# Inverse denominators on two sets of partitions, returned by two DMA queues, spread through two row halves of TensorE

## The reference

```python
score = exp(clip((K[src] * Q[dst] / sqrt(dh) * Eh).sum(-1), -5, 5))    # layer 0, 8 heads of 16
wV = segment_sum(V[src] * score, dst)
Z  = segment_sum(score, dst)
h  = x + (wV / (Z + 1e-6)).reshape(N, D)
x1 = layernorm(x + batchnorm(h))
e  = leaky_relu(a_src[src] + a_dst[dst]) ...                           # layer 1: attention, two linears
out = layernorm(x1 + layer1(x1))
```

## Time and profile before

| | before |
|---|---|
| median of three runs | 4573.03 us |
| the profiled execution | 4564.05 us, of which the span from first to last instruction is 4562.0 us |
| mean granted TensorE clock | 0.699 of full speed |
| busy share of the span: PE, DVE, ACT, POOL | 77%, 71%, 26%, 72% |

### The profile page before, as it was taken

The page is one execution under the profiler, slowest core; times in us unless marked ns, Lnnn a source line. Parts: engine busy times, 40 slices in busy tenths (PEclk is TensorE's granted clock), DMA queues, the critical chain, the costliest instruction groups (busy, mean ns, idle before and its releaser), DMA issues. The chain is left out here.

```text
span 4562.0 us, 84765 instructions
## 1 busy us (share of the span) xinstructions
PE 3498.3 (77%) x20796; PEld 2714.5 (60%) x20797; DVE 3235.4 (71%) x9533; ACT 1204.7 (26%) x4817; POOL 3274.2 (72%) x3437
## 2 busy tenths in 40 slices
PE   6787777778778777777889777777777777777778
PEld 5565555556556555565568655655555655556555
DVE  5877878887887878777548666666666666666657
ACT  3111111111111111111234333333333333333325
POOL 4777777777777777776567777777777777777752
PEclk9988988887898888988685555555555555555559
DMA  8666666666666666665343222222222222222224
GB/s 280 195 191 188 194 189 186 191 194 188 191 191 188 187 194 192 190 188 160 101 123 63 61 61 60 59 61 61 61 61 61 59 60 61 61 61 59 61 70 146
DMA packets 432619, 586.92 MB, mean 129 GB/s; under 512 B 210833, under 2 KB 290935, under 8 KB 431079
## 3 DMA queue, kind: packets, MB, share of 16 engines
q0 software_dynamic: 132880, 330.18, 27.5%
q1 hardware_dynamic: 297848, 248.72, 18.5%
q10 hardware_dynamic: 1840, 7.43, 0.4%
HBM read 551.16 MB, written 33.98 MB: 128 GB/s over the span
## 5 line engine op out<-in xcount | busy, mean ns | idle before, releaser
L1099 POOL DMA_INDIRECT xg<-xl_table,idx x1661 | 1590.3, 957 | 518.3 <-issue 498.3
L399 POOL DMA_INDIRECT kv_g<-kv_table,idx x1661 | 1575.4, 948 | 525.3 <-issue 504.5
L1164 PEld LDWEIGHTS ps_sum<-pw,xg 128*128 128x128 f32 x3328 | 741.0, 328 | 164.9 <-DVE pws L1305 164.9
L1164 PE MATMUL ps_sum<-pw,xg 128*128 128x64 f32 x3328 | 819.3, 428 | 3.8 <-DVE pws L1305 2.2
L1151 PE MATMUL ps_tops<-ident,top 128*64 128x128 f32 x832 | 286.1, 447 | 525.5 <-DVE top L1277 525.2
L467 PE MATMUL ps_sum<-kv_g,hot 128*64 128x136 f32 x3328 | 333.0, 328 | 455.8 <-issue 222.0
L449 PE MATMUL ps_pair<-w,eat 128*128 128x128 f32 x3328 | 599.9, 335 | 2.7 <-DMA eat<-in_edges 2.7
L1263 DVE SCALAR_TENSOR_TENSOR ps_lg<-raw 128x256 f32<-128x256 f32 x416 | 185.3, 445 | 573.4 <-ACT raw L1212 566.8
L1212 ACT ACTIVATE raw<-adw,xg 128x64 f32<-128x64 f32 x1664 | 440.8, 336 | 538.0 <-DMA xg<-xl_table,idx 537.8
L449 PEld LDWEIGHTS ps_pair<-w,eat 128*128 128x128 f32 x3328 | 506.5, 233 | 98.3 <-issue 98.3
L467 PEld LDWEIGHTS ps_sum<-kv_g,hot 128*64 128x64 f32 x3328 | 209.7, 154 | 560.8 <-issue 325.5
(11 more groups left out here) (164 smaller groups left out, 4982.5 us busy)
## 6 DMA issues: line engine op xcount, KB each, us to landing
eat<-in_edges SPq DMA_DIRECT2D x416, 256.0 KB
local<-local_table SPq DMA_DIRECT2D x832, 64.0 KB
kv_g<-kv_table,idx POOLq DMA_INDIRECT x1661
xg<-xl_table,idx POOLq DMA_INDIRECT x1661, 2.5
xw<-in_xt SPq DMA_DIRECT2D x416, 32.0 KB
adw<-ad_row SPq DMA_DIRECT2D x416, 32.0 KB, 4.4
kv_table<-kv_out SPq DMA_DIRECT2D x25, 512.0 KB, 5.0
xl_table<-xl SPq DMA_DIRECT2D x25, 264.0 KB, 2.7
```

Of the source, the lines that this page charges most:

```text
L399: nc.gpsimd.indirect_dma_start(out=kv[:, u, k, 0:2 * D], out_offset=None, in_=m["kv_table"], in_offset=bass.IndirectOffsetOnAxis(ap=idx[:, ...
L1099: nc.gpsimd.indirect_dma_start(out=xg[:, u, k], out_offset=None, in_=m["xl_table"], in_offset=bass.IndirectOffsetOnAxis(ap=idx[:, u // B, ...
L1164: nc.tensor.matmul(ps_sum[:, b, 0:W], xg[:, u, k, 0:D], pw[:, b, k], start=(k == 0), stop=(k == K - 1))
```

## The change

A second copy of the inverses stands on partitions 64 to 71 of `acc[:, 1]` (W = 64, H = 8), and `heads` exists on those partitions too. ScalarE returns each piece to partitions 0 to 7 as before, and SyncE returns the same piece to partitions 64 to 71 by a DMA of its own; `inv_back` of a piece counts to 32. Even groups are spread from partitions 0 to 7 and odd ones from 64 to 71. Their PSUM results rotate over the four buffers of `ps_rows`, and a call waits for `divide(g - 4)`. In SyncE's program `return_twin(0)` to `return_twin(2)` stand behind the four L826 DMAs, and `return_twin(3)`, with its wait for the fourth reciprocal, between the first and the second load of `third`.

```diff
-        heads = sb("heads", [H, D])
+        heads = sb("heads", [W + H, D])
+        twin_part = [acc[W:W + H, 1, first * G:end * G].rearrange("h (a n) -> h a n", a=DH) for first, end in DEN_PIECES]
             for piece in range(len(DEN_PIECES)):
                 sp.dma_start(inv_part[piece], den_part[piece]).then_inc(den_out[piece], 16)
+            def return_twin(piece):
+                sp.wait_ge(inverted, piece + 1)
+                sp.dma_start(twin_part[piece], inv_part[piece]).then_inc(inv_back[piece], 16)
+
+            for piece in range(3):
+                return_twin(piece)
             for piece, (first, end) in enumerate(PIECES):
-                sp.wait_ge(inv_back[piece], 16)
+                if piece == 1:
+                    return_twin(3)
+                sp.wait_ge(inv_back[piece], 32)
                 sp.dma_start(third[:, first * G:end * G], xt[:, first * G:end * G]).then_inc(xt_in[piece], 16)
...
             def spread_inv(g):
-                if g >= 2:
-                    pe.wait_ge(divided, g - 1)
-                nc.tensor.matmul(ps_wide[:, g % 2], heads[:], acc[0:H, 1, at(g, G)], start=True, stop=True).then_inc(inv_spread, 1)
+                side = slice(g % 2 * W, g % 2 * W + H)
+                if g >= 4:
+                    pe.wait_ge(divided, g - 3)
+                nc.tensor.matmul(ps_rows[:, g % 4], heads[side], acc[side, 1, at(g, G)], start=True, stop=True).then_inc(inv_spread, 1)
...
-            pe.wait_ge(heads_made, 1)
+            pe.wait_ge(heads_made, 2)
             for piece, (first, end) in enumerate(DEN_PIECES):
-                pe.wait_ge(inv_back[piece], 16)
+                pe.wait_ge(inv_back[piece], 32)
...
-            nc.vector.tensor_copy(heads[:].rearrange("p (b d) -> p b d", d=DH),
-                                  m["ident"][0:H, 0:H].unsqueeze(2).to_broadcast([H, H, DH])).then_inc(heads_made, 1)
+            for side in (0, W):
+                nc.vector.tensor_copy(heads[side:side + H].rearrange("p (b d) -> p b d", d=DH),
+                                      m["ident"][side:side + H, side:side + H].unsqueeze(2)
+                                      .to_broadcast([H, H, DH])).then_inc(heads_made, 1)
...
-                nc.vector.tensor_tensor(part, part, ps_wide[:, g % 2], ALU.mult).then_inc(divided, 1)
+                nc.vector.tensor_tensor(part, part, ps_rows[:, g % 4], ALU.mult).then_inc(divided, 1)
```

## The result

The change made the kernel slightly slower, by 0.16%. On the chip where both were timed, 22 runs each, the median went from 4574.27 to 4581.61 us: 7.34 us more, a ratio of 1.0016 with a 95% interval of 1.0010 to 1.0022. The forecast was 3.6 us more, within a range of -3.5 to +11 us. So sign, range and mechanism held, and the size was half of what came.

What follows compares the result with a forecast made beforehand. TensorE's spread matmuls bound the loop at 1.70 us a group; the halves' 7.0 us gain is lost to the delayed second load, ending 3.6 us later: 4573.0 + 3.6 = 4576.6 us, range 4569.5 to 4584 us.

Steps and rivals of the forecast that it cites:

- The bound and who is next: Spread loop: TensorE's matmuls bound it at 1.70 us a group; freed of them, VectorE and GpSimd allow about 1.23 us.
- The signs named for being right: L829 issues near 2175, 2188, 2189; GpSimd idle 10 us before its fourth add, then 1.23 us adds; VectorE awaiting GpSimd; TensorE idling.
- One sign named for being wrong: Second half of the layer work: its low-clock part not lasting about 15 us would count against the forecast.
- part 5: Clock in the second half, low for 14.80 us before: effect taken as 0, with 1.8 us gained or lost possible.
- Part 1: Spread matmuls: two row halves and four PSUM buffers overlap groups, 0.85 us each; at most 7.0 us saved.
- Part 2: Ahead of the first reciprocal: extra VectorE copy of heads, some 0.2 us, hidden in a 1.77 us DMA wait; costs nothing.
- Part 3: SyncE's queue ahead of the first load of third: twins of pieces 0 to 2 delay it 2.3 us, bounds 0 and 4.5.
- Part 4: return_twin(3) ahead of the second load of third: waiting for the fourth reciprocal makes the fourth add 10.5 us later, end 3.6 later.
- The sum: Whole kernel: 3.6 us slower, profiled execution 4564.05 to 4567.7 us, median of runs 4573.0 to 4576.6 us.
- "keeps its place" case: Second half's clock: rise stays at 2239.6 us while the half starts 3.6 us later, gaining 1.8 us.
- The rival of serial twins: Returns and twins serialize on the same DMA engines: high bound, +10.1 us, 4583.1 us; chance 0.10.
- The rival in which the halves' gain stays: Second piece of third lands early enough, by 2187: 7.0 us faster, 4566.0 us; chance 0.05.

Runs made afterwards that it cites:

- the kernel with one half: Changed kernel with return_twin(3) behind all loads of third and every group spread from partitions 0 to 7: stage's first half 58.38 us, median +0.3 us against before.
- twin 3 last: Changed kernel with return_twin(3) moved behind all three loads of third: stage's first half 54.03 us, median 5.2 us below the kernel before, 0.9990.
- the halves from group 15 on: Kernel before plus four buffers, twins of pieces 2 and 3 behind the loads, both halves from group 15: first half 52.22 us, median -2.7 of 5838 us, 0.9999.
- the wait alone: Kernel before plus only SyncE's wait for the fourth reciprocal between first and second load of third: first half 64.64 us, median +6.8 us, 1.0018.
- with nothing beside it: Changed kernel, SyncE also waiting until return 3 and twin 3 landed before the second load of third: first half 67.54 us, one run, 4568.12 us.
- twins 0 to 2 alone: Kernel before plus only SyncE's twins 0, 1 and 2, all groups spread from partitions 0 to 7: first half 62.01 us, median +2.3 us, 1.0004.
- the change again: Changed kernel, unaltered, run once more on a chip 28% slower for every kernel: first half 65.77 us, median +7.8 us of 5838 us, 1.0010.

## Why the prediction was right

- *The bound and who is next.* TensorE bounded the loop at 1.70 us a group, and GpSimd and VectorE came next at 1.23: the 22 adds took 27.00 us, forecast 27.1. The signs named for being right came: the late load, the long wait of GpSimd, adds back to back behind it. One sign named for being wrong came too, in part 5.
- *Part 1, the halves overlap.* Confirmed by the kernel with one half. But the 7.0 us named as their most were never on the table with this order; with twin 3 last 4.3 us came, and 6.1 with the halves from group 15 on. Of the page of the Trainium skill named there ("TensorEngine Tiling (Array Packing)"), the "up to twice" stands in its Overview, and its warning on PSUM evacuation is for a fourfold gain; here evacuation and GpSimd did become the bound.
- *Part 2, the second copy of `heads`.* 0.46 us for both, and VectorE still idles 1.35 us ahead of its first reciprocal. Nothing, as said.
- *Part 3, twins 0 to 2.* Forecast 2.3 us between bounds of 0 and 4.5; the first add came 2.9 us late (3.2 the second time). No row decided for the middle of the two bounds, and that it came this near is luck. Neither price drawn from the two pages of the Trainium skill, 0 us by "SBUF — State Buffer" (Door 1) and 4.5 us by "DMA: Bandwidth & Descriptors" (Rules for kernel authors), came: the twins neither ran for nothing on their other partitions nor took fully turns.
- *Part 4, the wait.* From the first add to the reciprocal's end 4.85 us were forecast, and 2191.74 + 1.73 - 2188.63 = 4.84 came; 0.65 us to the load's issue, and 0.70 came. The step that was mis-sized is the landing of the second load: 9.3 us forecast (2.0 + 6.1 + 1.1 + 0.1), 12.36 measured. Of the terms, the load itself with its fixed time was right: 8.4 us with the wait alone, 8.1 with nothing beside it, forecast 8.2. The 1.1 us for return 3 and twin 3 ahead of it is where it failed: they cost 4.0 us, close to the upper bound of 4.3. I took half a return, where the trace of before had small returns at 60 KB a us and no sign that the load could pass them. The runs show that it can pass return 3, but not with twin 3 ahead of it.
- *The sum.* 17.70 + 2.94 + 4.84 + 0.70 + 12.36 + 27.00 = 65.54 us, against a forecast 17.70 + 2.3 + 4.85 + 0.65 + 9.3 + 27.1 = 61.9: 3.0 of the missing 3.6 us are the landing, 0.6 the early twins.
- *Part 5, the clock.* Taken as 0, with 1.8 us either way. The low clock lasted 11.05 us of the second half instead of 14.8, not the "about 15" without which the mechanism was to count as wrong; at 0.49 us each that is 1.8 us gained in the profiled execution (77.56 us from the end of the first half to the last store, before 79.41). The sum is that of the "keeps its place" case, the mechanism isn't: the half began 7.2 us later and the rise came 3.5 us later, counted from the stage's first DMA. Nothing ties it to the change, though (last section).

The rival of serial twins came nearer than its chance of 0.10 says: its mechanism was right at return 3 and twin 3 and half right at twins 0 to 2. The rival in which the halves' gain stays is what the moved twin gives, though with 4.3 us instead of its 7.0.

## What to carry to other kernels

Before a DMA with a wait is put into a queue, list what is queued behind it and ask when the wait is met: here one wait, met 12 us late, held a load that had nothing to do with it, and with the DMA behind that wait it cost 11.5 us where the gain was 4.3. Small transfers into few partitions, ahead of a large one, cost it nearly their whole transfer here (4.0 us for 256 KB, which at 60 KB a us take 4.3), and behind it nothing; put them behind the large transfer that something waits for, and send only those that a later bound will use. And to price a large transfer with small ones ahead of it, add their times, unless a row shows them side by side.

## What the runs showed of the hardware

- Two row halves of TensorE overlap even when each uses 8 rows: a group took 1.71 us on one half (the kernel with one half) and 1.23 us, the pace of GpSimd, on two; with the wait for TensorE gone from the timeline, thirty matmuls of 512 columns take 19.24 us of busy time in the changed kernel, 0.64 us each at the granted 0.50, where before fifty took 43.52, 0.87 us each.
- The start of TensorE's high clock isn't tied to the row halves. The low clock (granted 0.50, 1.2 GHz) at the head of the second half lasted 9.41 us in one profile of the change and 11.05 in the other, 14.84 before and 16.18 us in the kernel with the halves from group 15. Without the halves it was as short in two profiles, 10.8 us with the wait alone and 9.7 with twins 0 to 2 alone. What sets it stays open. The two ends of that spread, the change again and the halves from group 15:

```profile
3027.10:3036.50 9.40, 8.47 (x24) 5.82 (x25) 2.30 (x5) 2.53 (x4) 1.46 (x1) 0.50 0.00 0
...
3001.20:3017.30 16.10, 15.19 (x47) 10.97 (x47) 3.74 (x8) 4.28 (x7) 2.91 (x2) 0.50 0.06 17
```

  From the end of the first half to the last store it took 76.78 us with the short one and 80.07 with the long one: 3.3 us for 6.8 us more at the low clock, 0.48 us each, as forecast from the earlier trace rows. In a comparison of single profiles this is noise of up to 3 us, half of what the change costs.
- In the last two runs every kernel was 28% slower, and both traces have a kind of wait that the others lack:

```profile
ACT third L1213 <- remote: 997.5, 164, 9.5
```

  A releaser called remote, 997.5 us at this line alone in the change again and 1026.0 in the other kernel, and at other lines of both layers too. Its cause is open. The first half of the stage between the layers took the change the same 65.8 us there as in its other profile, so the profile of one stage could still be read where the total could not.
